# A four-layer gated transformer on one core: VectorE's sums and maxima get steps of their own, and all steps a new order

## The chip, the cores and the metric

One core of a Trainium2 chip runs the whole program in one launch. The metric is the device time of that launch in microseconds (us), as the median of several runs.

## The reference

Sixteen batch elements x of 256 tokens by 256 features, each with a context of the same size, pass four layers. Every sub-block reads the layer-normed x and is added to x through a gate:

```python
x = x + tanh(g_xattn[0]) * L0_xattn(ln(x), ctx)        # differential attention, 16 x 2 heads of 8
x = x + tanh(g_ffn[0])   * L0_ffn(ln(x))               # 3 cycles of a small gelu net that twists x
x = x + tanh(g_xattn[1]) * L1_xattn(ctx, ln(x), mask)  # 8 heads of 64 over context and latents
x = x + tanh(g_ffn[1])   * L1_ffn(ln(x))               # mixture: 2 shared and 8 routed experts, top 2
x = x + tanh(g_xattn[2]) * L2_xattn(ln(x), ctx, ctx)   # 16 heads of 16
x = x + tanh(g_ffn[2])   * L2_ffn(ln(x))               # attention of 16 heads of 8, then 8 experts, top 2
x = x + tanh(g_xattn[3]) * L3_xattn(ln(x), ctx, ctx)   # one head of 256
x = x + tanh(g_ffn[3])   * L3_ffn(ln(x))               # relu net with quantised weights
```

A mixture is a sum of `gate_e * expert_e(x)` over its experts e; each attention is a softmax of scaled scores times values.

## The kernel before

Two elements are worked on at a time, in two slots with their own buffers; eight passes make sixteen elements. Everything that an element goes through is cut into named steps, such as `f1.up` (both first products of one expert of the first mixture) or `l0.exp` (two heads' turned scores). A step is a triple of name, element and number. There are 4408 of them, and 3216 of these fill one of three PSUM tiles w0, w1, w2 in turn (`take`, L507); before a tile is filled again, TensorE waits for the step that read it out. Attention products with values go into two further tiles o0 and o1.

The order of the steps is written out: each character of the string `ORDER` (L228) names one of 20 lists (10 a slot: main line, contexts, and lists set aside such as products with values, means, or the first scores of the next pass), and the next step of that list comes next. `SCHEDULE` (L276) is the result. TensorE, ScalarE, VectorE and GpSimd each walk through the same `SCHEDULE` and issue what their share of each step is; semaphores count the steps (`SIGNALS`, `READ`, `COUNT`). So on each engine the instructions stand in one fixed order, and an engine that waits holds up all that stands behind it. SyncE's loads of weights are a program of their own (L1570 to L1652), which waits for the steps that last used a buffer (`used`, L1589).

What the change and the prediction touch:

- Attention in l0, l2 and f2 (`spread_attention` on TensorE L551, VectorE L1158). `max` makes scores of two heads (L587) and VectorE reduces them to row maxima (L1184). When the last is there, VectorE splits the maxima into two parts in `mp` (L1197 to L1200), TensorE turns `mp` (`shift`, L595, transposes at L521), VectorE adds the result to the queries `qsp` (L1203), and the second product, `exp` (L604), already holds scores less the maximum. ScalarE takes exp (L937), TensorE multiplies with the values (`pv`, L671). The preparation of `mp` is part of the shift's step number 0, so VectorE does it at the place where TensorE's first shift product stands.
- The first mixture (`f1.up`, `f1.down`): two products (L537), ScalarE's silu (L1040), VectorE's product (L1452), the down product on TensorE (L547), and `add_to_x` (L1151 to L1156), two instructions at L1154 that add the gated result to x. The second mixture (`f2.up` L782, `f2.down` L792) splits its operands in two parts and ends in `add_to_x` too. The sum is part of the down's step.
- Norms (`ln`): VectorE takes statistics (L1117, L1120), an inverse root by ten small steps (L1126 to L1130), and normalises (L1148); TensorE then transposes (`xT`, L521), ScalarE copies (L875).
- Probabilities of l1 and l3: ScalarE's exp (L1080, L1087) and TensorE's transposes (L530).

## Time and profile before

| what | value |
|---|---|
| median of 3 runs | 4761.23 us (4758.1 to 4762.06) |
| profiled execution, its time | 4777.81 us |
| profiled execution, its span | 4776.0 us |
| TensorE busy | 4316.2 us, 90% |
| VectorE busy | 2936.9 us, 61% |
| ScalarE busy | 2099.3 us, 44% |
| GpSimd busy | 111.9 us, 2% |
| moved by DMA | 228 MB, 48 GB/s on average |

The span runs from the first to the last instruction in the trace; busy is the time in which an engine had at least one instruction under way. In the views below PE is TensorE's products, PEld its loads of the stationary operand, DVE VectorE, ACT ScalarE, SP SyncE; `w L521` is what an instruction of line 521 writes into a PSUM tile w. The clock is the share of full speed that TensorE was granted.

### The profile page before, as it was taken

Reading aid. Unit: us, or ns where it says so; the run is one execution under the profiler, and the core shown is the slowest. Engines: PE = TensorE matmul, PEld = TensorE weight load, DVE = VectorE, ACT = ScalarE, POOL = GpSimd, SP = SyncE. Lnnn points to the kernel's source line nnn. Section 1 sums busy time; section 2 is a strip of 40 time slices with the busy share of each in tenths; the row PEclk is TensorE's granted clock in tenths of the full one; section 3 lists DMA queues with packets and bytes.
Section 4 is the critical chain, followed back from the end, with each engine's and each line's share of the span. In section 5 each row is a group of like instructions: output and inputs, shape, how many; then the busy total and the mean of one; then the engine's idle time right before and its main releaser. Section 6 shows DMA issues by size and latency. Waiting matters only on the chain. (4 is left out here: it accounts for less than half of the span.)

```text
span 4776.0 us, 72965 instructions
## 1 busy us (share of the span) xinstructions
PE 4316.2 (90%) x28256; PEld 3254.7 (68%) x28256; DVE 2936.9 (61%) x7633; ACT 2099.3 (44%) x3432; POOL 111.9 (2%) x196
## 2 busy tenths in 40 slices
PE   7898998989989899898998989898899988999889
PEld 4575865759657586575965759666596676866668
DVE  6556676566655666566665666656566566665655
ACT  3534545343543435534355353553435525255242
POOL 0000000000000000000000000000000000000000
PEclk7998999979999899998999999999899999999889
DMA  2010510103101031010300102001020010300012
GB/s 93 1 42 1 200 48 1 51 19 115 36 10 42 19 115 36 14 38 23 119 27 14 38 27 115 27 14 38 27 115 27 14 38 27 115 27 14 29 45 102
DMA packets 51763, 228.00 MB, mean 48 GB/s; under 512 B 4832, under 2 KB 21216, under 8 KB 31584
## 3 DMA queue, kind: packets, MB, share of 16 engines
q1 hardware_dynamic: 51424, 223.33, 12.9%
q8 instruction: 230, 3.77, 0.3%
q14 instruction: 109, 0.89, 0.1%
HBM read 202.34 MB, written 20.97 MB: 47 GB/s over the span
## 5 line engine op out<-in xcount | busy, mean ns | idle before, releaser
L1184 DVE TENSOR_REDUCE mx<-w 128x4 f32<-128x1024 f32 x512 | 608.3, 1221 | 130.2 <-PE w L587 116.3
L937 ACT ACTIVATE pt_spread<-w 128x1024 f32<-128x1024 f32 x512 | 517.9, 1024 | 262.3 <-PE w L604 243.7
L671 PE MATMUL o<-pt_spread,va 128*32 128x256 f32 x4096 | 521.7, 398 | 13.6 <-ACT pt_spread L937 12.0
L883 ACT ACTIVATE oth<-w,res 128x256 f32<-128x256 f32 x656 | 277.6, 472 | 560.1 <-PE w L782 443.7
L537 PE MATMUL w<-xnT,stream 128*128 128x256 f32 x1792 | 423.4, 385 | 15.2 <-DVE tmp L1148 8.7
L537 PEld LDWEIGHTS w<-xnT,stream 128*128 128x128 f32 x1792 | 339.2, 192 | 67.6 <-DVE tmp L1148 10.7
L782 PE MATMUL w<-qodd,va_hi 128*128 128x256 f32 x2048 | 354.2, 286 | 2.9 <-ACT oth L883 1.5
L671 PEld LDWEIGHTS o<-pt_spread,va 128*32 128x32 f32 x4096 | 200.5, 112 | 182.1 <-issue 50.9
L1154 DVE SCALAR_TENSOR_TENSOR x<-w,gate,x 128x256 f32<-128x256 f32 x512 | 224.1, 479 | 161.2 <-PE w L792 135.5
L587 PE MATMUL w<-ksp,qsp 32*128 32x256 f32 (+1 forms) x2048 | 258.4, 364 | 53.5 <-DVE mx L1184 25.7
L782 PEld LDWEIGHTS w<-qodd,va_hi 128*128 128x128 f32 x2048 | 288.6, 190 | 14.5 <-ACT oth L883 2.8
L1438 DVE TENSOR_REDUCE mx<-w 128x2 f32<-128x1024 f32 x128 | 155.8, 1225 | 193.3 <-PE w L641 192.5
L587 PEld LDWEIGHTS w<-ksp,qsp 32*128 32x128 f32 (+1 forms) x2048 | 167.0, 218 | 152.4 <-DVE mx L1184 53.1
L604 PEld LDWEIGHTS w<-qsp,ksp 32*128 32x128 f32 (+1 forms) x2048 | 149.9, 191 | 170.1 <-issue 126.4
L604 PE MATMUL w<-qsp,ksp 32*128 32x256 f32 (+1 forms) x2048 | 242.5, 333 | 18.2 <-DVE qsp L1203 10.4
L537 PE MATMUL w<-xnT,res 128*128 128x256 f32 x768 | 226.1, 441 | 34.6 <-ACT xnT L875 19.6
L664 PE MATMUL o<-pt,va 128*65 128x256 f32 x1024 | 243.1, 384 | 5.0 <-ACT pt L875 4.9
L875 ACT ACTIVATE oth<-o 128x256 f32<-128x256 f32 (+1 forms) x384 | 147.2, 384 | 190.8 <-PE o L671 118.4
L1040 ACT ACTIVATE oth<-w 128x256 f32<-128x256 f32 x160 | 61.5, 384 | 361.0 <-PE w L537 361.0
L537 PEld LDWEIGHTS w<-xnT,res 128*128 128x128 f32 x768 | 158.9, 218 | 77.4 <-issue 31.1
L782 PE MATMUL w<-qodd,stream_lo 128*128 128x256 f32 x1024 | 206.2, 283 | 0.0
L547 PE MATMUL w<-stream,oth 128*128 128x256 f32 x640 | 169.4, 388 | 29.7 <-DVE oth L1452 29.7
(256 smaller groups left out, 7811.7 us busy)
## 6 DMA issues: line engine op xcount, KB each, us to landing
stream_lo<-split SPq DMA_DIRECT2D x56, 1024.0 KB, 4.8
va_hi<-split SPq DMA_DIRECT2D x56, 1024.0 KB, 6.9
stream<-in_moe_dram SPq DMA_DIRECT2D x80, 384.0 KB, 3.1
stream<-in_resident_dram SPq DMA_DIRECT2D x8, 2048.0 KB, 7.4
raw<-in_moe_dram SPq DMA_DIRECT2D x8, 1024.0 KB, 6.6
split<-va_hi SPq DMA_DIRECT2D x8, 1024.0 KB, 8.9
split<-stream_lo SPq DMA_DIRECT2D x8, 1024.0 KB, 11.1
stream<-in_resident_dram SPq DMA_DIRECT2D x8, 1024.0 KB, 4.8
```

The source lines that it names most:

```text
L537: mm = pe.matmul(w[:, col0 + j * T:col0 + j * T + T], weight[:, k, (m0 + j) * P:(m0 + j + 1) * P], act[:, k, :], start=(k == 0), stop=(k = ...
L547: mm = pe.matmul(w[:, o:o + n], act[:, k, tt * P:(tt + 1) * P], weight[:, k, :], start=(k == 0), stop=(k == kc - 1))
L587: mm = pe.matmul(w[:, a * 512 + tt * T:a * 512 + (tt + 1) * T], qsp[s][b:b + plan.rows, c, tt * P:(tt + 1) * P], ksp[s][b:b + plan.rows, c ...
L604: mm = pe.matmul(w[:, a * 512 + kt * T:a * 512 + (kt + 1) * T], ksp[s][b:b + plan.rows, c, kt * P:(kt + 1) * P], qsp[s][b:b + plan.rows, c ...
L664: mm = pe.matmul(o[0:L1_DIM + 1, 0:T], by_heads1(s)[:, kt, u, :], p[:, kt * T:(kt + 1) * T], start=(kt == 0), stop=(kt == KT - 1))
L671: mm = pe.matmul(o[g:g + 32, 0:T], by_heads(plan, s)[:, kt, plan.v_of(h), :], p[:, a * 512 + kt * T:a * 512 + (kt + 1) * T], start=(kt == ...
L782: mm = pe.matmul(w[:, j * T:(j + 1) * T], wt[:, k, j * P:(j + 1) * P], a[:, k, :], start=(n == 0), stop=(n == len(parts) - 1))
L883: h = act.activation(dst[:, c, :], w[:, c * T:(c + 1) * T], func, bias=bias[:, c:c + 1], **more)
L937: act.activation(exp_buffer(plan.name + ".exp", s, u), w[:, :], ACT.Exp, scale=scale).then_inc(S["s_P"], 1)
L1154: h = dve.scalar_tensor_tensor(x[s][:, tt, :], w[:, tt * stride:tt * stride + D], gate_ap(tt), x[s][:, tt, :], ALU.mult, ALU.add)
L1184: dve.tensor_reduce(mx[s][:, :, 2 * u:2 * u + 2].rearrange("p t a -> p a t"), w[:, :].rearrange("p (a t k) -> p a t k", a=2, t=TT), AX_X, ...
L1438: dve.tensor_reduce(mx[s][:, :, u], w[:, :].rearrange("p (t k) -> p t k", t=TT), AX_X, ALU.min)\
```

## The change

Two kinds of step are new. `f1.sum` and `f2.sum` (288 in all) are VectorE's `add_to_x` of the two mixtures, taken out of the down steps; the PSUM tile of the down is now free when the sum is done (`READER`). They go to a list set aside, so that they may stand anywhere behind their down. `l0.peak`, `l2.peak` and `f2.peak` (48 in all) are VectorE's preparation of `mp`, taken out of the first shift; they stay in the line of their attention, between the last max and the first shift. VectorE waits for the last sum of its element ahead of l2.ln and l3.ln. `ORDER` is new throughout and names 4744 steps. The instructions of each step are the same.

```diff
--- before.py
+++ after.py
@@ -112,7 +112,7 @@
     "s_soft": ("l1.soft", "l3.soft"), "s_P": ("l0.exp", "l1.exp", "l2.exp", "f2.exp"), "s_P3": ("l3.exp",),
     "s_pv": ("l0.pv", "l1.pv", "l2.pv", "f2.pv"), "s_back": ("l0.back", "l1.back", "l2.back", "f2.back"),
     "s_o": ("l0.norm",), "s_aT": ("l0.oT", "l1.oT", "l2.oT", "f2.oT"),
-    "s_xadd": ("l0.out", "l1.out", "f1.down", "l2.out", "f2.down", "f2.b2", "l3.pv", "f3.out"),
+    "s_xadd": ("l0.out", "l1.out", "f1.sum", "l2.out", "f2.sum", "f2.b2", "l3.pv", "f3.out"),
     "s_gm": ("f0.mean",), "s_gw": ("f0.g3",), "s_g": ("f0.g1", "f0.g2", "f0.g3"), "s_hid": ("f0.h1", "f0.h2", "f0.h3"),
     "s_tht": ("f0.t",), "s_cur": ("f0.turn",), "s_cT": ("f0.cT",),
     "s_kvT": ("l1.cT", "l1.xT"), "s_qhi": ("l1.q",), "s_k1hi": ("l1.kc", "l1.kl"), "s_qz": ("l1.q",), "s_k1": ("l1.kc", "l1.kl"), "s_v1": ("l1.vc", "l1.vl"),
@@ -126,7 +126,7 @@
     "l0.v": "s_v", "l2.v": "s_v", "f2.v": "s_v", **{n: "s_ksp" for n in SIGNALS["s_ksp"]}, **{n: "s_qsp" for n in SIGNALS["s_qsp"]},
     **{n: "s_mx" for n in SIGNALS["s_mx"]}, **{n: "s_qaug" for n in SIGNALS["s_qaug"]}, "l1.max": "s_soft", "l3.max": "s_soft",
     **{n: "s_P" for n in SIGNALS["s_P"]}, "l3.exp": "s_P3", **{n: "s_back" for n in SIGNALS["s_back"]},
-    **{n: "s_aT" for n in SIGNALS["s_aT"]}, **{n: "s_xadd" for n in SIGNALS["s_xadd"]}, "f0.g1": "s_g", "f0.g2": "s_g", "f0.g3": "s_g",
+    **{n: "s_aT" for n in SIGNALS["s_aT"]}, **{n.replace(".sum", ".down"): "s_xadd" for n in SIGNALS["s_xadd"]}, "f0.g1": "s_g", "f0.g2": "s_g", "f0.g3": "s_g",
     "f0.h1": "s_hid", "f0.h2": "s_hid", "f0.h3": "s_hid", "f0.t": "s_tht", "f0.cT": "s_cT", "l1.cT": "s_kvT", "l1.xT": "s_kvT",
     "l1.q": "s_qz", "l1.kc": "s_k1", "l1.kl": "s_k1", "l1.vc": "s_v1", "l1.vl": "s_v1", "f1.lg": "s_lg", "f2.lg": "s_lg",
     "f1.up": "s_up1", "f2.up": "s_gelu2", "f2.cTr": "s_cTr", "f2.mla": "s_mla", "l3.k": "s_qk3", "l3.q": "s_qk3", "l3.v": "s_v3",
@@ -136,7 +136,7 @@
 
 
 
-READER = {"l1.max": "l1.soft", "l3.max": "l3.soft"}
+READER = {"f1.down": "f1.sum", "f2.down": "f2.sum", "l1.max": "l1.soft", "l3.max": "l3.soft"}
 
 
 def steps_of(s, *names):
@@ -146,7 +146,7 @@
 
 def scores(plan, s):
     n = plan.name
-    return [(n + ".max", s, u) for u in range(plan.units)] + [(n + ".shift", s, c) for c in range(plan.shifts)]
+    return [(n + ".max", s, u) for u in range(plan.units)] + [(n + ".peak", s, 0)] + [(n + ".shift", s, c) for c in range(plan.shifts)]
 
 
 def values(plan, s):
@@ -169,7 +169,7 @@
 
 
 def experts(n, s, count):
-    return [(f"{n}.{what}", s, e) for e in range(count) for what in ("up", "down")]
+    return [(f"{n}.{what}", s, e) for e in range(count) for what in ("up", "down", "sum")]
 
 
 def slot_steps(s):
@@ -204,8 +204,8 @@
 
 
 LISTS = 10
-ASIDE = (("pv", "back"), ("mean", "g1", "g2", "g3"), ("init",))
-FIRST = ("l0.ln", "l0.xT", "l0.q", "l0.qs", "l0.max", "l0.shift")
+ASIDE = (("pv", "back"), ("mean", "g1", "g2", "g3", "sum"), ("init",))
+FIRST = ("l0.ln", "l0.xT", "l0.q", "l0.qs", "l0.max", "l0.peak", "l0.shift")
 
 
 def lists_of(s):
@@ -226,43 +226,46 @@
 
 
 ORDER = (
-    "B718B18IHB11B8II88I8I88888I8888888I88I8II188I0IBI0I5I50I050I5I0II5I05050I5I05A505AFA050F505050A5F5A2F5AFAFAFAF0AFFAF0AF0"
...
+    "B718B18IB118188IB8HI8888888888I88888B8III88II0I0II550I050I505I0I50I50I5I0550I5050I50I50II505A5AF2A5FAF0AFAFAFAFAFA0FFA0F"
...
 )
 
 
@@ -288,9 +291,9 @@
 
 
 COUNT = {sem: numbered(steps_named(*names)) for sem, names in SIGNALS.items()}
-COUNT["s_mp"] = numbered([x for x in SCHEDULE if x[0].endswith(".shift") and x[2] == 0])
+COUNT["s_mp"] = numbered([x for x in SCHEDULE if x[0].endswith(".peak")])
 COUNT["s_oT"] = numbered([x for x in SCHEDULE if x[0].endswith(".pv") and x[0] != "l3.pv" and PLANS[x[0][:2]].item_ends(x[2])])
-SHIFTED = [x[:2] for x in SCHEDULE if x[0] in ("l0.shift", "l2.shift", "f2.shift") and x[2] == 0]
+PEAKS = [x[:2] for x in SCHEDULE if x[0].endswith(".peak")]
 ITEM = numbered([x for x in SCHEDULE if x[0].endswith(".pv") and x[0] != "l3.pv" and PLANS[x[0][:2]].item_starts(x[2])])
 EXP_STEPS = [steps_named("l1.exp")] + [[x for x in steps_named("l0.exp", "l2.exp", "f2.exp") if x[1] % SLOTS == n] for n in range(SLOTS)]
 EXP_RING = {step: (ring, n) for ring, steps in enumerate(EXP_STEPS) for n, step in enumerate(steps)}
@@ -591,7 +594,7 @@
                 elif what == "shift":
 
                     w = take(st + ".shift", s, u)
-                    pe.wait_ge(*after("s_mp", st + ".shift", s))
+                    pe.wait_ge(*after("s_mp", st + ".peak", s))
                     filled(transpose_tokens(w, 4, lambda tt, j: mp[:, tt, (4 * u + j) * P:(4 * u + j + 1) * P]))
                 elif what == "exp":
 
@@ -1149,7 +1152,7 @@
                 return h
 
             def add_to_x(step, s, u, gate_ap, stride=D):
-                w = full(dve, step, s, u)
+                w = full(dve, step.replace(".sum", ".down"), s, u)
                 for tt in range(TT):
                     h = dve.scalar_tensor_tensor(x[s][:, tt, :], w[:, tt * stride:tt * stride + D], gate_ap(tt), x[s][:, tt, :],
                                                  ALU.mult, ALU.add)
@@ -1183,21 +1186,21 @@
                     w = full(dve, st + ".max", s, u)
                     dve.tensor_reduce(mx[s][:, :, 2 * u:2 * u + 2].rearrange("p t a -> p a t"),
                                       w[:, :].rearrange("p (a t k) -> p a t k", a=2, t=TT), AX_X, ALU.max).then_inc(S["s_mx"], 1)
+                elif what == "peak":
+                    dve.wait_ge(*after("s_mx", st + ".max", s, plan.units - 1))
+                    i = PEAKS.index((st + ".peak", s))
+                    if i:
+                        last, ls = PEAKS[i - 1]
+                        full(dve, last[:2] + ".shift", ls, PLANS[last[:2]].shifts - 1)
+                    m, hb = mx[s][:, :, 0:plan.heads], hib[:, :, 0:plan.heads]
+                    aug = AUG8 if plan.rows == 32 else AUG16
+                    g = mp[:, :, 0:plan.chunks * P].rearrange("p t (h r) -> p t h r", r=plan.rows)
+                    if plan.rows == 64:
+                        link(dve.memset(g[:, :, :, AUG8:AUG8 + 2], 0.0))
+                    link(dve.tensor_copy(hb, m))
+                    link(dve.tensor_scalar(g[:, :, :, aug], hb, -1.0, None, ALU.mult))
+                    dve.tensor_tensor(g[:, :, :, aug + 1], hb, m, ALU.subtract).then_inc(S["s_mp"], 1)
                 elif what == "shift":
-                    if u == 0:
-                        dve.wait_ge(*after("s_mx", st + ".max", s, plan.units - 1))
-                        i = SHIFTED.index((st + ".shift", s))
-                        if i:
-                            last, ls = SHIFTED[i - 1]
-                            full(dve, last, ls, PLANS[last[:2]].shifts - 1)
-                        m, hb = mx[s][:, :, 0:plan.heads], hib[:, :, 0:plan.heads]
-                        aug = AUG8 if plan.rows == 32 else AUG16
-                        g = mp[:, :, 0:plan.chunks * P].rearrange("p t (h r) -> p t h r", r=plan.rows)
-                        if plan.rows == 64:
-                            link(dve.memset(g[:, :, :, AUG8:AUG8 + 2], 0.0))
-                        link(dve.tensor_copy(hb, m))
-                        link(dve.tensor_scalar(g[:, :, :, aug], hb, -1.0, None, ALU.mult))
-                        dve.tensor_tensor(g[:, :, :, aug + 1], hb, m, ALU.subtract).then_inc(S["s_mp"], 1)
                     w = full(dve, st + ".shift", s, u)
                     q = qsp[s][:, 4 * u:4 * u + 4, :]
                     dve.tensor_tensor(q, q.bitcast(F32), w[:, :].rearrange("p (c t) -> p c t", t=T), ALU.add).then_inc(S["s_qaug"], 1)
@@ -1381,8 +1384,10 @@
                         dve.wait_ge(s_xs[s], 16 * (pass_of(s) + 1))
                         signal(normalise(x0[s], x0[s]), "s_xt", step, s)
                     else:
+                        if stage in ("l2", "l3"):
+                            dve.wait_ge(*after("s_xadd", *(("f1.sum", s, MOE1 - 1) if stage == "l2" else ("f2.sum", s, MOE2 - 1))))
                         signal(normalise(xt[s], x[s], stage == "l1"), "s_xt", step, s)
-                elif step in ("l2.v", "f2.v") or stage in ("l0", "l2", "f2") and what in ("k", "q", "max", "shift"):
+                elif step in ("l2.v", "f2.v") or stage in ("l0", "l2", "f2") and what in ("k", "q", "max", "peak", "shift"):
                     spread_attention(PLANS[stage], what, s, u)
                 elif what == "back":
                     back(PLANS[stage], s, u)
@@ -1450,7 +1455,7 @@
                     w = full(dve, step, s, u)
                     dve.wait_ge(*after("s_silu", step, s, u))
                     dve.tensor_tensor(oth[s][:, 1, :], w[:, 512:512 + T], oth[s][:, 0, :], ALU.mult).then_inc(S["s_up1"], 1)
-                elif step == "f1.down":
+                elif step == "f1.sum":
                     r = u - (MOE1 - MOE1_ROUTED)
                     add_to_x(step, s, u, lambda tt: tg[:, 5:6] if r < 0 else gate[s][:, tt, r:r + 1])
 
@@ -1490,7 +1495,7 @@
                         link(dve.tensor_copy(ob_hi[s][:, c:c + 2, :], oth[s][:, c:c + 2, :]))
                         h = dve.tensor_tensor(oth_lo[s][:, c:c + 2, :], oth[s][:, c:c + 2, :], ob_hi[s][:, c:c + 2, :].bitcast(F32), ALU.subtract)
                     h.then_inc(S["s_up2"], 1)
-                elif step == "f2.down":
+                elif step == "f2.sum":
                     add_to_x(step, s, u, lambda tt: gate[s][:, tt, u:u + 1])
 
                 elif step == "l3.v":
```

Two places in the order show what moved. The first is on TensorE, in the third pass, around the shift of slot 0 in the third layer's attention. Lines of the new kernel are three higher from here on: 587 is 590 (scores for maxima), 521 is 524 (transposes), 574 is 577 (spreading the queries of slot 1), 537 is 540 (projection of slot 1's queries), 604 is 607 (exp). Before:

```order
L587 MATMUL w1<-ksp0_59,qsp0 128x256 x4
L587 MATMUL w2<-ksp0_59,qsp0 128x256 x4
L587 MATMUL w0<-ksp0_59,qsp0 128x256 x4
L574 MATMUL w1<-hl1,sel16q 128x256 x8
L574 MATMUL w2<-hl1,sel16q 128x256 x8
L521 MATMUL w0<-res,mp 128x128 x8
L521 MATMUL w1<-res,mp 128x128 x8
L587 MATMUL w2<-ksp1_62,qsp1 128x256 x4
L587 MATMUL w0<-ksp1_62,qsp1 128x256 x4
```

With the change:

```order
L590 MATMUL w0<-ksp0_59,qsp0 128x256 x4
L590 MATMUL w1<-ksp0_59,qsp0 128x256 x4
L590 MATMUL w2<-ksp0_59,qsp0 128x256 x4
L540 MATMUL w0<-xnT1,res 128x256 x4
L524 MATMUL w1<-res,mp 128x128 x8
L524 MATMUL w2<-res,mp 128x128 x8
L577 MATMUL w0<-hl1,sel16q 128x256 x8
L577 MATMUL w1<-hl1,sel16q 128x256 x8
L607 MATMUL w2<-qsp0,ksp0_59 128x256 x4
L590 MATMUL w0<-ksp1_62,qsp1 128x256 x4
```

Between the last scores of slot 0 and the shift (`res,mp`) two spreading steps of slot 1 stood; now the projection of slot 1's queries stands there, and both spreading steps follow the shift.

The second is on VectorE, in the third pass, at the end of slot 0's part of the first mixture. L1154 (now L1157) is a sum, L1452 (now L1457) the gating product, BN_STATS the start of `l2.ln`. Before:

```order
L1154 SCALAR_TENSOR_TENSOR x0<-w2,gate0,x0 128x256 x2
L1452 TENSOR_TENSOR oth0<-w0,oth0 128x256
L1154 SCALAR_TENSOR_TENSOR x1<-w1,gate1,x1 128x256 x2
L1452 TENSOR_TENSOR oth1<-w2,oth1 128x256
L1154 SCALAR_TENSOR_TENSOR x0<-w0,gate0,x0 128x256 x2
L1452 TENSOR_TENSOR oth0<-w1,oth0 128x256
L1154 SCALAR_TENSOR_TENSOR x1<-w2,gate1,x1 128x256 x2
L1154 SCALAR_TENSOR_TENSOR x0<-w0,gate0,x0 128x256 x2
L1117 BN_STATS stats<-x0 128x6 x2
```

With the change:

```order
L1457 TENSOR_TENSOR oth1<-w1,oth1 128x256
L1157 SCALAR_TENSOR_TENSOR x0<-w2,gate0,x0 128x256 x2
L1457 TENSOR_TENSOR oth0<-w0,oth0 128x256
L1157 SCALAR_TENSOR_TENSOR x1<-w1,gate1,x1 128x256 x2
L1157 SCALAR_TENSOR_TENSOR x0<-w2,gate0,x0 128x256 x2
L1457 TENSOR_TENSOR oth1<-w0,oth1 128x256
L1457 TENSOR_TENSOR oth0<-w1,oth0 128x256
L1157 SCALAR_TENSOR_TENSOR x1<-w2,gate1,x1 128x256 x2
L1457 TENSOR_TENSOR oth1<-w0,oth1 128x256
L1157 SCALAR_TENSOR_TENSOR x0<-w1,gate0,x0 128x256 x2
L1157 SCALAR_TENSOR_TENSOR x1<-w2,gate1,x1 128x256 x2
L1120 BN_STATS stats<-x0 128x6 x2
```

Sums and gating products took turns. Now a sum sometimes stands behind two gating products or another sum, and between slot 0's last sum and its norm there is one sum of slot 1.

## Rows read from the trace of the kernel before

**Rows 1.** The page's table of engines, and the clock of the core.
```profile
PE 4316.2 (90%) x28256; PEld 3254.7 (68%) x28256; DVE 2936.9 (61%) x7633; ACT 2099.3 (44%) x3432; POOL 111.9 (2%) x196
...
core 0: 4776.0 us, clock 0.948
```

**Rows 2.** Waits of TensorE: total us, times, longest us.
```profile
PE w L521 <- DVE xt L1148: 42.1, 34, 4.7
PE w L547 <- DVE oth L1452: 29.7, 37, 5.4
PE w L587 <- DVE mx L1184: 25.7, 52, 2.5
PE w L521 <- DVE mp L1200: 24.6, 23, 7.1
PE w L537 <- ACT xnT L875: 21.9, 27, 2.4
PE w L537 <- ACT oth L883: 20.8, 25, 1.4
...
PE w L530 <- ACT turned L1080: 10.8, 13, 2.4
...
PE w L521 <- DMA cx<-in_ctx_dram: 10.4, 1, 10.4
PE w L530 <- ACT kvT L1080: 9.8, 10, 2.2
...
PE w L530 <- ACT oth L1087: 6.3, 7, 1.5
```

**Rows 3.** Windows, third pass: us, busy us by engine (count), clock, DMA share, GB/s.
```profile
1297.00:1362.00 65.00, 49.35 (x255) 33.85 (x255) 42.01 (x163) 28.69 (x56) 4.36 (x6) 0.89 0.00 1
1544.00:1612.00 68.00, 58.60 (x408) 39.19 (x408) 44.35 (x100) 30.25 (x39) 3.45 (x4) 0.85 0.05 16
1686.00:1800.00 114.00, 112.62 (x925) 104.28 (x924) 79.36 (x140) 38.07 (x79) 0.00 (x0) 1.00 0.32 121
```

**Rows 4.** Timeline, last sum of slot 0: start, us, instructions, idle before.
```profile
1537.80 1.10 PE L547 MATMUL w<-stream,oth 128*128 128x256 f32 x4 [0.26 <-DVE oth L1452]
...
1539.01 0.88 DVE L1154 SCALAR_TENSOR_TENSOR x<-w,gate,x 128x256 f32<-128x256 f32 x2 [0.56 <-PE w L547]
...
1544.04 0.63 PE L521 MATMUL w<-res,xt 128*128 128x128 f32 x4 [0.81 <-DVE xt L1148]
```

**Rows 5.** Timeline, shift of slot 0, third attention, third pass.
```profile
1569.96 2.35 DVE L1184 TENSOR_REDUCE mx<-w 128x4 f32<-128x1024 f32 x2
...
1572.75 0.20 DVE L1199 TENSOR_SCALAR mp<-hib 128x32 f32<-128x32 bf16 x1
1572.99 0.21 DVE L1200 TENSOR_TENSOR mp<-hib,mx 128x32 f32<-128x32 bf16 x1
...
1573.35 0.45 PE L521 MATMUL w<-res,mp 128*128 128x128 f32 x1 [0.90 <-DVE mp L1200]
```

**Rows 6.** Windows, second pass, around its third attention; columns as in rows 3.
```profile
970.00:980.00 10.00, 8.00 (x42) 6.11 (x42) 5.07 (x11) 4.17 (x5) 0.00 (x0) 0.50 0.00 0
980.00:990.00 10.00, 9.16 (x52) 6.00 (x52) 7.26 (x7) 2.99 (x3) 0.00 (x0) 0.50 0.01 2
```

**Rows 7.** Waits of VectorE on the sums, and the page's group of sums.
```profile
DVE x L1154 <- PE w L792: 135.5, 113, 4.2
...
DVE x L1154 <- PE w L547: 97.8, 71, 6.5
...
L1154 DVE SCALAR_TENSOR_TENSOR x<-w,gate,x 128x256 f32<-128x256 f32 x512 | 224.1, 479 | 161.2 <-PE w L792 135.5
```

**Rows 8.** DMA issues of weights: KB each, median us to landing.
```profile
stream_lo<-split SPq DMA_DIRECT2D x56, 1024.0 KB, 4.8
va_hi<-split SPq DMA_DIRECT2D x56, 1024.0 KB, 6.9
stream<-in_moe_dram SPq DMA_DIRECT2D x80, 384.0 KB, 3.1
```

75 lines of the change are left out of this document (39 added, 36 removed).

## The prediction

> **What bounds the kernel now.** I read the page's table of engines first, then the clock, the waits of TensorE, the busy time by stage, and last two places in the timeline. TensorE is busy 4316.2 of 4776.0 us, VectorE 2936.9 [rows 1]. So TensorE is the bound, and what a new order can win is its idle time, 4776.0 - 4316.2 = 460 us, and what the clock lost. The idle time is not one wait but very many short ones: the ten kinds quoted in [rows 2] hold 202 us in 229 waits, the longest of those for another engine 7.1 us. It sits in certain stages [rows 3]: in the third pass TensorE idles 15.7 us of the 65 of the first feed-forward net, 9.4 of the 68 around the third attention, and 1.4 of the 114 of the second mixture. In the second mixture the change can win next to nothing, whatever place the second mixture's sums get.
>
> The clock is the second cost. The granted mean is 0.948 [rows 1]; with two levels, 2.4 and 1.2 GHz, the lower held for 2 x 0.052 x 4776 = 497 us. It held from 970 to 990 us, for example, where TensorE was busy 17.2 of 20 us [rows 6].
>
> Two places show what a wait is made of. At the end of the first mixture [rows 4] the last down product ends at 1538.90 us, VectorE adds it (0.88), takes statistics, inverse root and normalises, and TensorE's transposes start at 1544.04: the hand-off needs 5.1 us, other products covered 4.3, TensorE stood 0.81. At the shift [rows 5] VectorE's last reduce ends at 1572.31, its four small steps on the maxima end at 1573.20 and TensorE starts at 1573.35 after 0.90 us idle. With the reduce itself (1.2 us) the hand-off needs about 2.5 us from the last product of scores.
>
> **The change, part by part.** No instruction is added, removed or resized: 288 sums (two instructions each, 479 ns [rows 7]) and 48 preparations stay. The wait added before l2.ln and l3.ln asks for a sum that VectorE has itself finished by its own order; its price lies between 0 and one wait instruction on 32 steps, some 32 x 0.04 = 1 us at the gap between two chained steps in [rows 5]; nobody waits for it in particular, and I take 0. No load is moved in SyncE's program, but its waits follow the downs. I measured in both orders how much TensorE work lies between the down that frees a buffer and the next use of it: for the second mixture at least 8.9 us before and 9.0 after in the passes that load, for the first 3.6 and 3.6. Landings take 4.8, 6.9 and 3.1 us [rows 8], and TensorE waited for no weight before (only 10.4 us for the first context [rows 2]), so I take 0 here too; at worst one late load of 1 us in each pass, 8 us.
>
> What is left is where steps stand. For every hand-off from TensorE over another engine back to TensorE I counted in both orders the TensorE work that stands between (the cover), with the length that each kind of step has in this trace, and took as short a hand-off whose cover is below its need. The cover starts at the last product that VectorE must still take in before the step, not only at the step's own.
> - Norms after a residual (need 5.1 us, 80 of them): missing cover 78 us before, 54 after. TensorE waits 42.1 us for them [rows 2]. 42.1 x (1 - 54/78) = 13 us.
> - Preparation of maxima (need 2.5, 48 of them): 32 us missing before, 15 after; 24.6 us of waits [rows 2] x (1 - 15/32) = 13 us. This is the new step's own work: in the first order block the projection of the other slot's queries now covers the preparation, in place of two spreading steps.
> - First mixture's gating (need 1.1, 160): short 36 times before and 37 after, 17 and 15 us missing; 29.7 x 2/17 = 4 us. The sum moves behind the next gating only sometimes: in 158 of 288 cases it still stands right behind its down.
> - Turned probabilities (l1.exp, l3.exp): missing 17 us before, 4 after; waits 10.8 + 9.8 + 6.3 = 26.9 us [rows 2] x 13/17 = 20 us. Only the new search does this.
> - Transposed activations (L537 behind ACT xnT): missing 24 and 16; 21.9 x 8/24 = 7 us.
> - Shift added to the queries, before the first exp: missing 9.9 and 7.6, at most 2.3, I take 2 us.
> - PSUM banks held by maxima (L587 behind mx): over all kinds of bank 173 us missing before, 160 after; 25.7 x 13/173 = 2 us.
> - The gelu chain of the first net (its first link is the row of 20.8 us): missing 47 and 44, 3 us. Queries and keys spread over rows: missing 13 and 18, of which I take 4 as a loss. Copies of products and transposes of attention outputs: a loss of 3. The norm of l1.out and f1.ln misses 14 us more, but in this trace it was hardly waited for; I take 0 and keep 14 for the range.
>
> Sum: 13 + 13 + 4 + 20 + 7 + 2 + 2 + 3 - 4 - 3 = 57 us. Not all of it can last. Where TensorE no longer stands, the cover of the next hand-off, which its idling had stretched, becomes shorter, and part comes back there. Bounds from rows: nothing lasts, 0; all lasts, 57. I take two thirds, 38, nearer the upper end, because the count finds what the trace shows: 24 short preparations against 23 waits, 36 short gatings against 37 [rows 2].
>
> The clock: idle time falls by 38/460, 8%. Nothing given back is one bound; the other is that the 497 us at 1.2 GHz fall by as much, 40 us, of which half is won, 20 us. I take 10. So 48 us in all. The profiled execution took 4777.8 us by the times, 1.8 over its span, and would take 4730. The median of the three runs, 4761.2, lies 16.6 below it; I forecast against the median: 4761 - 48 = **4713 us**.
>
> The Trainium skill, TensorE: Matmul & The Clock Gate, section HAM oscillation, names long idle gaps as what makes the clock fall. By that rule shortening many short waits gives no clock back, and the sum would be 38 us, 4723. The rows speak for some gain: in [rows 6] the clock is at its lower level, 0.50, while TensorE is 80 and 92% busy.
>
> **The rivals.** A measurement of this kernel can tell about 0.2%, 9.5 us, from no change.
> - *The waits go and stay gone, with the clock.* 57 + 20 = 77 us, and gains at places the count doesn't see, up to half as much again: 4646 to 4684, at its middle 4665. For it: the missing cover falls in each of the eight passes, and the kinds of [rows 2] are only 202 of the 460 us; the rest stands at places where queues on VectorE and ScalarE matter, which freer places should relieve. Against: the same slack serves several chains at once.
> - *The new places are hardly used.* The sums stay behind their downs (158 of 288), the second mixture has 1.4 us of idle per pass to win, and only the search's remainder lasts, one third of 57, 19 us, no clock: 4742. For it is the count of the gating, 36 short before and 37 after.
> - *Nothing.* What one stage wins the next gives back: 4761. The spread queries and l1.out's norm, which got worse, speak for it.
> - *VectorE's order turns against TensorE (slower).* VectorE takes its steps in the written order; it stood 135.5 us in 113 waits for the second mixture's products and 97.8 us for others with later steps behind [rows 7]. A sum with a place of its own can stand ahead of a norm. In the second order block the third pass does this: l2.ln of slot 0 now follows the sum of slot 1's product 7, which lasts 1.0 to 1.1 us [rows 4] and stands right behind slot 0's last down. If each of the 80 norms and 48 preparations waited 1 us longer that is 128 us; it outweighs the 48 us above when more than 48 of the 128 do. With 72 of them, 72 us against 48: 24 us slower, 4785. Against it: counted with this head of line, norms still miss less cover than before (54 against 78 us).
>
> The Trainium skill, same page, the table of the queue depths, says of VectorE "strict FIFO", of TensorE that only weight loads are pulled ahead. It speaks for the last rival's mechanism, and the trace agrees, with the 135.5 us above; by it alone, with all 128 hit and nothing won, the time would be 4761 + 128 = 4889.
>
> **How the numbers follow.** Forecast 0.42, larger gain 0.22, small gain 0.20, nothing 0.08, slower 0.08. The first three are faster by over 0.2%: 0.84; same 0.08, slower 0.08. The range takes the larger gain down to 4655, and upwards the small gain, nothing, and with the 14 us of l1.out's norm up to 4775; it leaves out the lowest part of the larger gain and most of the slower case, some 0.13 together.
>
> **What would show it.** TensorE busy about the same in the two runs save for the clock (4290 to 4320 us), idle about 415 us, mean clock 0.95 to 0.96. PE behind DVE mp near 12 us (from 24.6), behind DVE xt near 29 (42.1), behind turned, kvT and oth of L1080 and L1087 together near 7 (26.9), behind ACT xnT near 15 (21.9). VectorE busy unchanged at 2937 us. The forecast is wrong if TensorE's idle time stays above 450 us, or if a wait for a weight load appears. If waits behind mp and xt fall as said and the span doesn't, the slack was shared; if they rise, it is VectorE's queue.

## The result, and the profile after

| | before | with the change |
|---|---|---|
| median of 4 runs, us | 4761.65 | 4679.09 (4675.16 to 4686.74) |
| ratio to before, 95% interval | | 0.9829 [0.9812, 0.9846] |
| profiled execution, its time | 4777.81 | 4675.16 |
| its span | 4776.0 | 4673.4 |
| TensorE idle in it (span less busy) | 459.8 | 393.1 |

The change makes the kernel 83 us, 1.7%, faster. The forecast was 4713: the sign was right, and the size was 48 where 83 came. The profile's own table of engines says where it came from, with the clock below it:

```profile
PE 4280.3 (92%) x28256; PEld 3232.2 (69%) x28256; DVE 2938.2 (63%) x7633; ACT 2090.1 (45%) x3424; POOL 112.3 (2%) x196
```

```profile
core 0: 4673.4 us, clock 0.957
```

Against [rows 1] the same 28256 products take 36 us less, and idle time is 66.7 us less. The profiled execution of before was 16.2 us over its median, and that of the change 3.9 under its own. The other executions of before, beside the experiments, show what this is: their clock lies between 0.948 and 0.954, and the longest spans are those of the lowest clock. At the medians about 16 of the 36 us are left. So I estimate that of the 83 us 67 are idle time and 16 are clock; this takes the idle time of the two profiled executions for that of the medians, which were not traced. VectorE's busy time is what it was, as nothing was removed.

The waits of TensorE, total us, times, longest us:

```profile
PE w L550 <- DVE oth L1457: 36.2, 40, 4.5
PE w L524 <- DVE xt L1151: 28.9, 21, 4.4
PE o L674 <- ACT pt_spread L940: 19.4, 25, 1.6
PE w L540 <- ACT oth L886: 18.3, 24, 1.0
PE w L540 <- ACT xnT L878: 16.6, 22, 2.4
...
PE w L590 <- DVE mx L1187: 15.6, 37, 1.2
PE w L607 <- DVE qsp L1206: 14.3, 22, 1.5
...
PE w L590 <- ACT pt_spread L940: 11.8, 15, 1.6
PE w L577 <- issue: 11.5, 11, 6.2
...
PE w L524 <- DMA cx<-in_ctx_dram: 10.1, 1, 10.1
...
PE w L533 <- ACT turned L1083: 8.2, 12, 1.2
...
PE w L533 <- ACT kvT L1083: 5.2, 5, 2.2
...
PE w L524 <- DVE mp L1202: 1.9, 3, 0.7
...
PE w L533 <- ACT oth L1090: 1.3, 3, 0.8
```

Three rows of before that [rows 2] leaves out:

```profile
PE o L671 <- ACT pt_spread L937: 12.0, 22, 1.2
PE w L604 <- DVE qsp L1203: 10.4, 22, 0.8
PE w L587 <- ACT pt_spread L937: 3.6, 7, 0.9
```

Most kinds fell. Of those shown four rose: the gating product (36.2 from 29.7), the products with values behind ScalarE's exp (19.4 from 12.0), scores behind the same (L590 behind pt_spread, 11.8 from 3.6), and exp behind the queries with the shift added (L607, 14.3 from 10.4). One line must be read with care. Of the 24.6 us behind `mp` in [rows 2], 7.1 were a single wait at 64 us from the start, where VectorE is still busy with one-time set-up. It is not gone: it stands now at 59 us, 6.2 us long, as the longest of the 11 waits called "issue" at L577, as the timeline of the start shows:

```profile
59.11 1.22 PE L577 MATMUL w<-hl,sel8q 32*128 32x256 f32 x8 [6.24 <-issue]
```

Without it the preparations cost 17.5 us in 22 waits before and 1.9 in 3 after.

The stretches that answer to [rows 3], with the same columns, at the places of the same steps:

```profile
1277.00:1341.00 64.00, 52.43 (x286) 35.60 (x285) 45.83 (x182) 30.10 (x58) 3.36 (x4) 0.95 0.00 1
1522.00:1584.00 62.00, 53.80 (x396) 35.64 (x396) 46.09 (x114) 29.81 (x38) 3.37 (x4) 0.86 0.00 1
1657.00:1771.00 114.00, 110.90 (x922) 103.66 (x915) 78.69 (x156) 37.99 (x78) 0.68 (x2) 1.00 0.30 113
```

The first net idles 11.6 us (15.7 before), the third attention 8.2 (9.4) in a stretch that is 6 us shorter, because TensorE has other work in it, and the second mixture 3.1 (1.4). Each of the eight passes became shorter, by 5 to 22 us, measured from the end of one pass's first net to that of the next. The gain has no one place.

### The profile page after: what moved, and what is told of

Same layout as the page of the kernel before. It is cut to its first block, busy times and chain, and to the rows that moved or that the text cites. A ratio compares the mean times of both kernels' runs of the same rounds, so it can differ in the third digit from the quotient of the medians.

```text
span 4673.4 us, 72994 instructions
## 1 busy us (share of the span) xinstructions
PE 4280.3 (92%) x28256; PEld 3232.2 (69%) x28256; DVE 2938.2 (63%) x7633; ACT 2090.1 (45%) x3424; POOL 112.3 (2%) x196
## 3 DMA queue, kind: packets, MB, share of 16 engines
q1 hardware_dynamic: 51424, 223.33, 13.2%
## 4 chain that ended last, share of the span: by engine, by line
PE 78%; DVE 13%; ACT 6%; issue 3%; DMA 0%; DVEq 0%; SPq 0%; ACTq 0%
PE w L540 18%; PE w L550 11%; PE o L674 10%; PE w L795 8%; PE w L785 8%; PE w L607 4%; PE o L667 4%; PE w L524 4%; PE w L590 3%; DVE mx L1187 3%; PE w L533 2%; PE w L642 2%; PE w L686 1%; ACT pt_spread L940 1%; ACT oth L886 1%
## 5 line engine op out<-in xcount | busy, mean ns | idle before, releaser
L674 PE MATMUL o<-pt_spread,va 128*32 128x256 f32 x4096 | 537.1, 406 | 19.7 <-ACT pt_spread L940 19.4
L886 ACT ACTIVATE oth<-w,res 128x256 f32<-128x256 f32 x656 | 277.4, 471 | 567.9 <-PE w L785 460.1
L590 PE MATMUL w<-ksp,qsp 32*128 32x256 f32 (+1 forms) x2048 | 258.8, 359 | 50.4 <-DVE mx L1187 15.6
L1157 DVE SCALAR_TENSOR_TENSOR x<-w,gate,x 128x256 f32<-128x256 f32 x512 | 223.8, 479 | 121.1 <-PE w L795 96.8
L607 PEld LDWEIGHTS w<-qsp,ksp 32*128 32x128 f32 (+1 forms) x2048 | 153.6, 192 | 178.6 <-issue 130.7
L607 PE MATMUL w<-qsp,ksp 32*128 32x256 f32 (+1 forms) x2048 | 249.1, 335 | 17.9 <-DVE qsp L1206 14.3
L590 PEld LDWEIGHTS w<-ksp,qsp 32*128 32x128 f32 (+1 forms) x2048 | 167.7, 215 | 138.8 <-DVE mx L1187 40.4
L540 PE MATMUL w<-xnT,res 128*128 128x256 f32 x768 | 222.7, 436 | 25.7 <-ACT xnT L878 14.7
L550 PE MATMUL w<-stream,oth 128*128 128x256 f32 x640 | 172.0, 393 | 36.6 <-DVE oth L1457 36.2
```

The costliest lines, as they stand in the source:

```text
L540: mm = pe.matmul(w[:, col0 + j * T:col0 + j * T + T], weight[:, k, (m0 + j) * P:(m0 + j + 1) * P], act[:, k, :], start=(k == 0), stop=(k = ...
L550: mm = pe.matmul(w[:, o:o + n], act[:, k, tt * P:(tt + 1) * P], weight[:, k, :], start=(k == 0), stop=(k == kc - 1))
L590: mm = pe.matmul(w[:, a * 512 + tt * T:a * 512 + (tt + 1) * T], qsp[s][b:b + plan.rows, c, tt * P:(tt + 1) * P], ksp[s][b:b + plan.rows, c ...
L607: mm = pe.matmul(w[:, a * 512 + kt * T:a * 512 + (kt + 1) * T], ksp[s][b:b + plan.rows, c, kt * P:(kt + 1) * P], qsp[s][b:b + plan.rows, c ...
L674: mm = pe.matmul(o[g:g + 32, 0:T], by_heads(plan, s)[:, kt, plan.v_of(h), :], p[:, a * 512 + kt * T:a * 512 + (kt + 1) * T], start=(kt == ...
L886: h = act.activation(dst[:, c, :], w[:, c * T:(c + 1) * T], func, bias=bias[:, c:c + 1], **more)
```

## Experiments

All kernels below were timed beside runs of before on the same chip; each ratio is to those, with its 95% interval. Where two kernels are compared in us, their ratios times 4761 are subtracted, unless they ran together. The experiments with places put the changed order of steps through a small function:

```python
def arranged(order):
    order = list(order)
    sums = [x for x in order if x[0].endswith(".sum")]
    peaks = [x for x in order if x[0].endswith(".peak")]
    ...
    return order

SCHEDULE = arranged(in_order())
```

The line of dots is the edit; `behind(order, a, b)` and `ahead(order, a, b)` move step a next to step b. Since sums and preparations issue on VectorE alone, moving one leaves TensorE's, ScalarE's and GpSimd's own orders untouched.

### The new order with the old places: a_glued, a_sums_glued, a_peaks_glued

```diff
+    for x in sums:        # a_glued, a_sums_glued: right behind their down
+        behind(order, x, down_of(x))
+    for x in peaks:       # a_glued, a_peaks_glued: right ahead of their first shift
+        ahead(order, x, (x[0].replace(".peak", ".shift"), x[1], 0))
```

> The new order with every sum put back right behind its down and every preparation of maxima right ahead of its first shift, so only the search's order of the old steps remains. Theory A (the new places carry a good part): waits behind mp go from 1.9 us back to 10 to 25, the time rises by 15 to 30 us over the changed kernel's 4679, to 4694 to 4709. Rival B (the search alone carries it): 4679 to 4684, waits behind mp may rise but other waits fall.

> The new order with only the sums put back right behind their downs. Theory A: the sums' places carry little, since 158 of 288 are there already: 0 to 6 us slower than the changed kernel, 4679 to 4685. Rival: the deferred sums free VectorE for gating products, then this loses 10 us or more and waits of L550 behind oth rise above 36 us. A second rival: deferred sums hurt the gating (36.2 us of waits against 29.7 before), then this one is faster than 4679.

> The new order with only the preparations of maxima put back right ahead of the first shift. Theory A: waits behind mp rise from 1.9 to 10 to 25 us, the time by 8 to 20 us, to 4687 to 4699. Rival (slack is shared): the waits behind mp rise, but the next waits fall, and the time stays within 4 us of 4679.

With the changed kernel they make a table of two by two, all with the new order of TensorE:

| | sums glued | sums in own places |
|---|---|---|
| preparations glued | a_glued 4780.17, 1.0044 [1.0031, 1.0057] | a_peaks_glued 4777.72, 1.0039 [1.0026, 1.0052] |
| preparations in own places | a_sums_glued 4694.44, 0.9859 [0.9845, 0.9873] | the change, 0.9829 [0.9812, 0.9846] |

Places of sums are worth 14 us (0.9859 against 0.9829) with the preparations free, and 2 us without, which their intervals do not tell from nothing. Places of preparations are worth 88 to 100 us. For a_sums_glued the rival had it right, and its profile says so: norms and gating wait 8.7 and 5.1 us longer than in the changed kernel.

```profile
PE w L573 <- DVE oth L1480: 41.3, 42, 5.4
PE w L547 <- DVE xt L1174: 37.6, 26, 4.5
```

For the preparations none of the quoted theories had the size. Theory and rival of a_glued both had it faster than before; it is slower. In the profile of a_peaks_glued one wait stands out:

```profile
PE w L547 <- DVE mp L1225: 72.5, 30, 11.0
```

```profile
PE 4330.6 (90%) x28256; PEld 3270.5 (68%) x28256; DVE 2941.3 (61%) x7633; ACT 2089.7 (44%) x3424; POOL 112.2 (2%) x196
```

Of its 72.5 us, 11.0 are the one-time wait of the start. The other 61.5 us come with no VectorE instruction being longer. Why shows in the timeline. First the changed kernel, slot 0's shift in the third attention of the third pass:

```profile
1540.83 3.75 PE L540 MATMUL w<-xnT,res 128*128 128x256 f32 x8 [0.43 <-DVE mx L1187]
1543.03 0.11 DVE L1199 MEMSET mp<- 128x64 f32 x1
...
1543.62 0.21 DVE L1202 TENSOR_TENSOR mp<-hib,mx 128x32 f32<-128x32 bf16 x1
...
1544.38 2.01 PE L524 MATMUL w<-res,mp 128*128 128x128 f32 x16
...
1544.62 0.84 ACT L886 ACTIVATE hl<-w,res 128x256 fp32r<-128x256 f32 x2 [7.79 <-PE w L540]
1545.57 0.88 DVE L1174 SCALAR_TENSOR_TENSOR hl<-w,res,hl 128x256 fp32r<-128x256 f32 x2 [1.73 <-PE w L524]
```

Then the same place with the preparation glued to the shift (lines are 23 higher):

```profile
1568.92 3.19 PE L563 MATMUL w<-xnT,res 128*128 128x256 f32 x7
...
1572.15 0.84 ACT L909 ACTIVATE hl<-w,res 128x256 fp32r<-128x256 f32 x2 [7.79 <-PE w L563]
1573.10 0.88 DVE L1197 SCALAR_TENSOR_TENSOR hl<-w,res,hl 128x256 fp32r<-128x256 f32 x2 [2.62 <-ACT hl L909]
1573.94 0.11 DVE L1222 MEMSET mp<- 128x64 f32 x1
...
1574.54 0.21 DVE L1225 TENSOR_TENSOR mp<-hib,mx 128x32 f32<-128x32 bf16 x1
...
1574.90 2.98 PE L547 MATMUL w<-res,mp 128*128 128x128 f32 x16 [2.78 <-DVE mp L1225]
```

Eight products of the other slot's queries (`w<-xnT,res`) cover the shift in both; the second view begins behind the first of them, hence x7. But VectorE must also read what they make: with ScalarE it turns them into `hl`. Glued, the preparation stands behind that on VectorE, so VectorE first waits for the very products that were to cover it, for ScalarE's copy (1572.15), for its own step (1573.10), and only then begins on the maxima, at 1573.94. TensorE stood 2.78 us. In the changed kernel the preparation is done at 1543.83, while the covering products still run, and the shift starts at 1544.38 without a wait. The trace shows the same over all 48 shifts. At 30 of them at least one VectorE step stands in the new order between the preparation and the first shift. At 29 of these the idle time ahead of the shift grew, by 70.6 us in all, the 11.0 of the start among them. At the thirtieth the step is the norm of a context, 17 instructions that wait for no product of TensorE, and the shift gained nothing, nor did the 18 shifts with no step between. So it is a step that waits which costs, not a step as such.

### The old order with early preparations: b_peaks_early

The order of before, decoded as before, with each preparation as a step of its own right behind the last max.

```diff
+    for x in peaks:
+        behind(order, x, (x[0].replace(".peak", ".max"), x[1], PLANS[x[0][:2]].units - 1))
```

> The old order, sums behind their downs as before, and only the preparations moved up, right behind the last max of their attention. Theory A: waits behind mp fall from 24.6 us to 5 or less and the time by 8 to 20 us from 4762, to 4742 to 4754, without any search. Rival (slack is shared): waits behind mp fall, but the time stays within 4 us of 4762.

Measured: 4766.65, ratio 1.0013 [1.0003, 1.0022]. The place alone wins nothing.

```profile
PE w L548 <- DVE xt L1175: 44.7, 36, 5.4
...
PE w L548 <- DVE mp L1226: 12.7, 16, 1.4
...
PE w L614 <- DVE nlam L1399: 10.4, 1, 10.4
```

The rival was the nearer one. The waits behind `mp` fall from 24.6 to 12.7, but 7.1 of that is the start's wait, which moves to another row (L614 behind `nlam`, 10.4) and grows; the real saving of 4.8 us is eaten by waits for norms (44.7 from 42.1) and small ones, so that all idle time is 458.7 us against 459.8. In the old order 29 of the 48 shifts had no VectorE step at all between last max and shift, so there was nothing to move the preparation ahead of.

### Early preparations in the new order, and a norm's place: a_peaks_first, c_norm_first

```diff
+    for x in peaks[1:]:   # a_peaks_first
+        behind(order, x, (x[0].replace(".peak", ".max"), x[1], PLANS[x[0][:2]].units - 1))
+    for n, last in (("l2", ("f1.sum", MOE1 - 1)), ("l3", ("f2.sum", MOE2 - 1))):   # c_norm_first
+        for s in range(ELEMENTS):
+            behind(order, (n + ".ln", s, 0), (last[0], s, last[1]))
```

> The new order, with every preparation of maxima but the first moved up to right behind the last max of its attention. If the places that the search chose between max and shift matter beyond being ahead of what waits, this is slower by 5 us or more; theory A says that only what stands behind a waiting step hurts, waits behind mp are 1.9 us already, and so it stays within 4 us of 4679.

> The new order, with l2.ln and l3.ln moved up to right behind their own element's last sum, ahead of the other slot's sums and gating products that stood between. Theory A (the other slot's sum ahead of a norm costs TensorE its product's 0.9 us and the sum's 0.88, the mechanism of the slower rival): waits of the transposes behind the norm fall from 28.9 us by 5 to 12, and the time by 3 to 12 us, to 4667 to 4676. Rival (the search put them there because the gating product that then comes later is needed first): waits of L550 behind oth rise by as much and the time is 4679 to 4690.

a_peaks_first: 4677.18, ratio 0.9804 [0.9790, 0.9818], its profiled span 4676.5 against 4673.4, its idle time 394.4 us against 393.1. In time it lies within 2 us of the changed kernel, as theory A said. By the ratios it would be 12 us faster, with a before of 4769.64 on that chip; the two intervals overlap, so no difference is shown. Where exactly a preparation stands has no weight that these runs can tell, as long as it stands ahead of what reads the cover.

c_norm_first: 4699.24, ratio 0.9853 [0.9838, 0.9868], 11 us slower than the changed kernel by the ratios and 22 slower than a_peaks_first beside it. Theory and rival both had it faster than this. The edit moves more than its expectation says: 15 of the 32 norms change place, and only 3 of these had a sum in between. The others had mainly steps of attention, such as the next pass's first scores, which VectorE now does behind a norm of some fifteen instructions. That is where waits rose:

```profile
PE w L548 <- DVE xt L1175: 29.1, 19, 4.7
...
PE w L614 <- DVE mx L1211: 19.4, 38, 3.6
```

The scores' wait for their banks is 15.6 in the changed kernel; the norms' own wait, 28.9 there, does not fall in sum. So the total says little of the sum ahead of `l2.ln`, which the second order block shows and which I had put down as a possible harm. The timeline of that place does. First the changed kernel, then two lines of c_norm_first:

```profile
1522.00 0.63 PE L524 MATMUL w<-res,xt 128*128 128x128 f32 x4 [0.82 <-DVE xt L1151]
```

```profile
1528.76 2.00 PE L574 MATMUL w<-res,ctxT 128*128 128x256 f32 x8 [2.01 <-DVE x L1181]
...
1530.60 0.60 PE L548 MATMUL w<-res,xt 128*128 128x128 f32 x4
```

With the norm first its transposes no longer wait 0.82 us. But the other slot's sum now stands behind the norm and holds its PSUM tile, and TensorE waits 2.01 us for that tile. The sum ahead of the norm costs 0.8 us there, and taking it away costs more.

### What one microsecond of waiting costs: e_delay

Two further memsets ahead of each of the 48 preparations; they write a scratch tile that nothing reads.

```diff
+                    for _ in range(2):
+                        link(dve.memset(tmp[:, :], 0.0))
```

> The changed kernel, with two memsets of 128 x 512 on VectorE ahead of each of the 48 preparations of maxima, some 0.5 us each. It prices a wait. Theory C (a wait costs its length and again about half of it through the clock): of 48 us added to VectorE some 25 to 40 reach TensorE as waits behind mp, and the time rises by 1.3 to 1.6 times what these waits rise. Rival (a wait costs its own length or less, since slack is shared): the ratio is 1 or below.

Measured: 4729.29, ratio 0.9917 [0.9902, 0.9931]; beside a_peaks_first it is 52 us slower, by the ratio to before and that of the changed kernel 42.

```profile
L1199 DVE MEMSET tmp<- 128x512 f32 x96 | 46.6, 485 | 16.5 <-DVE tmp L1199 8.3 <-DVE mx L1187 6.9 <-PE w L607 0.7
```

```profile
PE w L524 <- DVE mp L1204: 34.2, 35, 1.9
```

```profile
PE 4301.8 (91%) x28256; PEld 3244.1 (69%) x28256; DVE 2985.7 (63%) x7729; ACT 2089.9 (44%) x3424; POOL 112.2 (2%) x196
```

46.6 us of work on VectorE became 32.3 us of waits for `mp` (34.2 less 1.9) and all of TensorE's idle time grew by 32.6; but its busy time grew too, by 21.5 us for the same products, and the clock is 0.950. A microsecond of waiting cost 1.3 us (42 by 32.6, from the ratios) to 1.7 us (54.1 by 32.6, from the profiled spans), as theory C said. a_peaks_glued agrees: idle time 62.8 us over that of the changed kernel, time 100 us over it by the ratios, 1.6 each.

### Can the cover be put into the old order by hand? b_cover, b_cover_glued, n_cover

If a shift needs other products between last max and shift, and the preparation must stand ahead of what reads them, an edit of the old order should do it (theory D of the quoted texts): draw steps of the other slot from behind the shift to ahead of it until 2.5 us stand there.

```diff
+    for x in peaks[1:]:
...
+            for y in moved:               # the other slot's next steps, until 2.5 us are between
+                ahead(order, y, shifts[0])
...
+        behind(order, x, last)            # b_cover, n_cover: right behind the last max
+        ahead(order, x, shifts[0])        # b_cover_glued instead: right ahead of the shift
```

> The old order with one hand-made edit instead of a search: before a first shift with less than 2.5 us of TensorE work since the last max, later steps of the other slot are drawn ahead of it until 2.5 us stand there (20 places short, 12 after), and the preparation stands right behind the last max. Theory D (place and cover only work together, and this is what the search used): waits behind mp fall from 24.6 us to 12 or less, and the time is 4740 to 4754 against 4762 to 4766 with the places alone. Rival (what is drawn ahead is missed as cover elsewhere): 4760 or more.

> The same TensorE order as b_cover, but every preparation right ahead of its shift, as in the kernel before. 28 of the 48 then have a step of VectorE between the last max and the preparation. Theory D: VectorE waits there for the cover's own product, waits behind mp rise by some 1 to 2.5 us at each of 10 or more places, and this is 15 to 50 us slower than b_cover. Rival: the place of the preparation hardly matters, within 5 us of b_cover.

> The new order with the same edit (20 short places become 5) and every preparation but the first right behind the last max. Waits behind mp are only 1.9 us in the changed kernel, so little is left there: theory D expects the time within 6 us of 4679, or slower where the drawn steps were cover elsewhere. Faster by over 8 us would mean that the search left room at the shifts.

| kernel | order | median | ratio to before |
|---|---|---|---|
| b_cover | old, drawn, preparations early | 4791.84 | 1.0057 [1.0043, 1.0071] |
| b_cover_glued | the same, glued | 4831.06 | 1.0133 [1.0118, 1.0149] |
| n_cover | new, drawn, early | 4718.77 | 0.9906 [0.9891, 0.9921] |

b_cover, then b_cover_glued:

```profile
PE w L654 <- DVE qsp L1253: 26.7, 27, 2.6
...
PE o L721 <- ACT pt_spread L987: 17.6, 31, 1.2
...
PE w L571 <- DVE mp L1249: 8.7, 4, 7.1
```

```profile
PE w L571 <- DVE mp L1249: 45.6, 21, 7.4
...
PE w L654 <- DVE qsp L1253: 24.1, 26, 1.4
```

Two things follow. The pair confirms the mechanism in another order: with covering steps of the other slot in place, gluing the preparation costs 36.9 us of waits (45.6 against 8.7) and 39 us of time, where in the order of before, without such steps, its place was worth nothing. And cover isn't made, it is moved: b_cover wins 15.9 us at `mp`, but exp now waits 26.7 us for the queries with the shift added (10.4 in the kernel before) and the products with values wait 17.6 (12.0), most likely because the drawn steps had covered those. It is 27 us slower than before, as its rival said. n_cover shows the same with next to nothing to win: the same drawing in the new order raises that wait of exp to 25.5 us (14.3) and costs 37 us against the changed kernel by the ratios, 49 against a_peaks_first, which it differs from by the drawing alone. That a gain needs all places weighed together, as a search does and this edit doesn't, fits these runs but is not shown by them.

### Can idle products lift the clock? d_fill4, d_fill_few

```diff
+            def idle_work(w):
+                for _ in range(4):
+                    pe.matmul(w[:, 0:P], first_row[:, 0:P], first_row[:, 0:P], start=True, stop=True)
                 w = take("f0." + what, s, c)
+                idle_work(w)
```

The same stands ahead of the transposes of every norm but l0's: 368 places, 1472 products, whose result the real product overwrites. d_fill_few puts 352 of them at the steps whose waits are longest, on top of a_peaks_first.

> The changed kernel, with four small bf16 products of 128 columns (results overwritten) put on TensorE ahead of the wait in every step of the first feed-forward net and ahead of the transposes behind six norms: 368 places. Theory C (TensorE's idle pieces hold its clock down, and half of the loss is the clock's): mean clock rises from 0.957 to 0.965 or more; the products cost at most 368 x 0.2 to 0.4 us = 80 to 150 us where nothing waits and nothing where TensorE idles, so the time lies between 4650 and 4700. Rival (the clock does not answer to such work): mean clock stays at 0.957 and the time rises by 20 to 80 us.

> The new order with early preparations (4677 by itself), and idle work on TensorE only where the waits are long on average: 6 small bf16 products ahead of g3, 2 ahead of h2 in the first net, 5 ahead of the transposes behind the norms of the third attention and of the attention inside the second mixture's block (352 products in all against 1472). Theory C: clock from 0.956 to 0.959 or more and the time 4660 to 4676. Rival (the products cost what the clock gives back): 4677 to 4690.

d_fill4: 4695.23, ratio 0.9846 [0.9832, 0.9859]; d_fill_few: 4677.36 (4665 to 4699), 0.9817 [0.9793, 0.9842]. The rows are of d_fill4:

```profile
L523 PE MATMUL w<-first_row 128*128 128x128 bf16 x1472 | 146.0, 222 | 25.1 <-DVE k L1446 9.6 <-DVE mx L1194 7.6 <-DVE x L1164 3.8
```

```profile
PE 4345.8 (93%) x29728; PEld 3305.7 (70%) x29728; DVE 2938.7 (63%) x7633; ACT 2094.1 (45%) x3424; POOL 112.6 (2%) x196
...
core 0: 4690.7 us, clock 0.962
```

The clock rises to 0.962, the highest of all kernels, and the time at the lower level falls from 2 x 0.043 x 4673 = 402 to 2 x 0.038 x 4691 = 356 us. That is less than the 0.965 of theory C. The products have 146 us of busy time, more than half of it under way together with other products, so that TensorE's busy time rises by 65.5 us, while its idle time falls by only 48.2 (344.9 from 393.1). The net is a loss: 8 us by the ratios, 18 beside a_peaks_first. With a quarter of them nothing is lost or won that its runs can tell. No version here beats the changed kernel by more than its measurement can tell.

## Why the prediction was right and where it failed

The terms against what the waits of the two profiles say:

| term | foreseen us | measured us |
|---|---|---|
| norms after a residual (xt) | 13 | 13.2 |
| preparation of maxima | 13 | 15.6, and 0.9 at the start |
| first mixture's gating | 4 | -6.5 |
| turned probabilities (3 rows) | 20 | 12.2 |
| transposed activations (xnT) | 7 | 5.3 |
| banks held by maxima (mx) | 2 | 10.1 |
| gelu chain (L886) | 3 | 2.5 |
| shift added to the queries (qsp) | 2 | -3.9 |
| queries and keys spread over rows (hl) | -4 | 5.9 |
| idle time in all | 38 | 66.7 |
| clock | 10 | 16 by the estimate above (36 in the profiled executions) |

Right were: TensorE as the bound and idle time as what can be won; the counts of missing cover for the norms (to a fifth of a microsecond), the activations (within 2) and the preparations (within 4); nothing from the second mixture; VectorE's busy time; no wait for a weight load. Of the signs that were named ahead, the clock (0.957) and the waits behind `xt` and `xnT` came as said. The waits behind `mp` fell to 1.9 and not to 12, those of the turned probabilities to 14.7 and not to 7, TensorE's busy time to 4280.3, below the 4290 named, and idle time to 393 and not to 415.

**The discount was the failing step.** I made 57 us and let two thirds of it last, 38, where 66.7 came. The first seven rows of the table were foreseen at 62 us and measured 53: 86% lasted. That this sum is so near is in part luck, since the gating was 10.5 us and the turned probabilities 7.8 us short, and the banks 8.1 us over. The other 13 us came, net, from elsewhere. The spread queries, of which I had counted a loss of 4 us, won 5.9 (L577 behind `hl`, 1.2 from 7.1), and GpSimd's output (L524 behind `ob`, 7.5 from 12.6), which I had not counted, won 5.1; the two waits for ScalarE's exp, 15.6 us longer together, went against it. My reason for the discount was that a hand-off's cover shrinks when TensorE no longer stands elsewhere. Something of the kind is seen where one thing is moved in an order otherwise kept, in b_peaks_early and b_cover. My counts were made on both whole orders, and there it was the smaller effect.

Two readings under the term of the preparations were off. The 24.6 us held the start's wait, which no cover shortens; without it the same working gives 17.5 x 17/32 = 9 us. And the need of 2.5 us was set high, as [rows 5] give 1573.35 - 1572.31 + 1.2 = 2.2.

**Costing the places one by one was wrong as a way of thinking**, though it did little harm to the number. The part on the preparations put 13 us on "the new step's own work". The runs give no such price: in the old order the new place is worth -6 us, in the new order 88 to 100. The new order as such, with the old places, is 0.4% slower than before. Neither half is a gain, together they are 83 us. What the place buys is that a product whose result VectorE must read may serve as cover. The old order has a VectorE step between last max and shift at 19 of the 48 shifts, the new one at 31. In a_peaks_glued, TensorE's idle time apart from `mp` is 4786.5 - 4330.6 - 72.5 = 383 us, against 435 before (459.8 - 24.6): 52 of the 66.7 us of idle time won lie in other kinds of wait, and the preparation's place is what keeps `mp` from taking it back.

**The clock** was priced by one argument, half of 20 us, and came out at 16. e_delay measures what I lacked: added waits of at most 1.9 us cost 1.3 to 1.7 times their length. The rule that I set beside it, the Trainium skill, TensorE: Matmul & The Clock Gate, section HAM oscillation, names long idle gaps; taken as the whole rule it would give no clock for short waits. Here 32.6 us more of short waits took the granted mean from 0.957 to 0.950, and 62.8 us took it to 0.940. In this kernel the measurement decides against taking it so.

**The rivals.** The larger gain, 4665, was nearer than the forecast. Its reason was that freer places relieve queues which the count doesn't see. For the rows of banks and of `hl`, which fell well beyond what was foreseen, this is not so. a_glued has the old places, and both are as low there, `hl` at 1.3 us and the banks in this row:

```profile
PE w L615 <- DVE mx L1212: 15.3, 37, 1.1
```

They come with the order of the other steps. "The new places are hardly used" judged by the sums, 158 of 288 behind their down; this was the wrong step to look at, since the sums' places carry 14 us or less and those of the 48 preparations 88 to 100. The slower case had its mechanism right, a step ahead of another on VectorE: it is what a_peaks_glued shows, with 2.78 us at one shift, and the Trainium skill, TensorE: Matmul & The Clock Gate, the table of the queue depths, with its "strict FIFO" for VectorE, agrees with that trace. But in the changed kernel it works the other way: the new places take VectorE's steps out of such queues.

**Open** stays how much of the 83 us the search would have found without steps of their own for the preparations, since an order searched for the old lists was not made here. The runs show that this order needs the new places, not that no order could do without them. And c_norm_first's loss was read from its waits and one place, not taken apart further.

## What to carry to other kernels

Where engines follow one written order, the place of a short step matters as soon as the work that is to cover a hand-off also feeds the engine that must do the step: put the step ahead of the cover's own reader. Judge a new place and a new order together, each alone can be worth nothing or less; and if the count of missing cover was made on the final order, be slow to discount it again: here 86% of it lasted. Price a wait of a kernel near TensorE's bound above its length, by a delay experiment like e_delay, since the clock takes its share.

## What was not expected of the hardware

Many short waits, added, lower the granted clock. Changed kernel: idle 393 us, clock 0.957. With 32.6 us more of it, in waits of at most 1.9 us (e_delay): 0.950. With 62.8 us more (a_peaks_glued): 0.940. With 48 us less, filled by products of no use (d_fill4): 0.962. But these four share one order, and across orders the sum of idle time does not tell the clock: a_peaks_glued idles 455.9 us and the kernel before 459.8, and their clocks are 0.940 and 0.948, over all executions 0.937 to 0.946 and 0.948 to 0.954. So something else about the waits, such as their place or their length, must matter too; no run here took that apart.

Executions of one and the same kernel differ in the clock: a_peaks_glued ran with spans from 4767.8 us at 0.946 to 4793.4 at 0.937. By these means the lower level held for 2 x 0.054 x 4767.8 = 515 us and 2 x 0.063 x 4793.4 = 604 us, and half of the difference, 44 us, is more than the 25.6 us between the spans. So the clock can carry the whole spread; that it does is not shown, since one of these executions alone was traced.
